# Convolution block: fc2 and projection in four column tiles, the sum in sequence quarters, stored and read back as channels

## What is computed

```python
mid = jax.nn.silu(xn @ fc1_w + fc1_b) @ fc2_w + fc2_b
...
o = o / jnp.linalg.norm(o, axis=-1, keepdims=True)
o = o + mid
o = o.transpose(0, 2, 1, 3).reshape(B, L, Cc)
o = o @ proj_w + proj_b
...
x = x + _L0_conv_ref(_gn(x), ...)
t = _to_tokens(x)
t = t + _L1_attn_ref(_ln_t(t), ...)
t = t + _L1_ffn_ref(_ln_t(t), ...)
```

## Time and profile before

| | |
|---|---|
| time, median of 3 executions | 2920.16 us (2918.62 to 2920.73) |
| profiled execution, its own time | 2919.42 us |
| its span, first to last instruction | 2917.7 us |
| mean granted TensorE clock | 0.977 |
| busy: TensorE / VectorE / ScalarE / GpSimd | 94% / 79% / 69% / 40% |
| convolution block | from about 35 to 1009 us |
| causal attention | to about 2437 us |
| projection and FFN | to the end |

### The profile page before, as it was taken

How to read it: one execution, slowest core, us unless ns; L and a number is a source line. 1 busy time by engine, 2 the same in 40 slices (tenths; PEclk the granted TensorE clock), 3 DMA queues, 4 the chain that set the end, 5 groups by cost and what they waited for, 6 DMA issues and landing times. The chain is left out here.

```text
span 2917.7 us, 86416 instructions
## 1 busy us (share of the span) xinstructions
PE 2750.0 (94%) x29306; PEld 1683.2 (58%) x29306; DVE 2300.3 (79%) x4591; ACT 2020.9 (69%) x3943; POOL 1156.5 (40%) x1999
## 2 busy tenths in 40 slices
PE   3899999999999499999999999999999996899996
PEld 2555555555554266666666666666666664455553
DVE  4576766766666399999999999999999993678997
ACT  1677777777776367777777777777777774577775
POOL 0153434434444444444444444444444431224445
PEclk9999999999999689999999999999999998999998
DMA  1113232332332476666666666666666663334555
GB/s 34 36 63 107 83 113 82 107 110 78 113 113 66 132 127 118 118 117 117 117 117 117 117 117 117 117 117 117 117 117 117 117 114 82 98 99 136 147 139 155
DMA packets 923408, 316.04 MB, mean 108 GB/s; under 512 B 848785, under 2 KB 906418, under 8 KB 923314
## 3 DMA queue, kind: packets, MB, share of 16 engines
q1 hardware_dynamic: 921970, 313.59, 47.6%
q10 hardware_dynamic: 1344, 1.18, 0.1%
HBM read 113.35 MB, written 99.88 MB: 73 GB/s over the span
## 5 line engine op out<-in xcount | busy, mean ns | idle before, releaser
L965 DVE TENSOR_REDUCE at_unit_max<-at_ps_queries 128x1 f32<-128x512 f32 (+4 forms) x2304 | 1135.0, 549 | 89.0 <-PE at_ps_queries L853 86.6
L928 ACT ACTIVATE at_probs<-at_ps_keys 128x512 f32<-128x512 f32 x1344 | 743.3, 603 | 387.6 <-PE at_ps_keys L868 383.0
L853 PE MATMUL at_ps_queries<-at_turned 96*128 96x128 bf16 (+3 forms) x3456 | 634.4, 274 | 33.1 <-DMA at_turned<-at_spread 32.3
L868 PE MATMUL at_ps_keys<-at_turned 128*128 128x128 bf16 (+3 forms) x3456 | 648.7, 275 | 1.8 <-ACT at_probs L928 1.5
L803 POOL TENSOR_TENSOR at_v<-at_stacks,at_one 128x128 f32<-128x128 f32 x192 | 76.9, 401 | 813.0 <-DMA at_stacks<-qkv_rows 813.0
L888 PE MATMUL at_ps_values<-at_probs,at_v 128*32 128x128 f32 x10752 | 373.4, 276 | 6.5 <-ACT at_probs L928 6.4
L868 PEld LDWEIGHTS at_ps_keys<-at_turned 128*128 128x128 bf16 x3456 | 237.8, 97 | 239.5 <-ACT at_probs L928 88.6
L853 PEld LDWEIGHTS at_ps_queries<-at_turned 96*128 96x128 bf16 x3456 | 289.3, 97 | 124.4 <-DMA at_turned<-at_spread 34.0
L888 PEld LDWEIGHTS at_ps_values<-at_probs,at_v 128*32 128x32 f32 x10752 | 269.5, 109 | 120.5 <-ACT at_diag_probs L928 70.2
L928 ACT ACTIVATE at_diag_probs<-at_ps_keys 128x512 f32<-128x512 f32 x384 | 208.6, 595 | 8.2 <-PE at_ps_keys L868 5.3
L822 POOL TENSOR_SCALAR_AFFINE_SELECT at_diag_probs<-at_diag_probs 128x1024 f32<-128x1024 f32 x192 | 210.6, 1097 | 0.0
(11 more groups left out here) (212 smaller groups left out, 5028.3 us busy)
## 6 DMA issues: line engine op xcount, KB each, us to landing
qkv_rows<-cb_packed SPq DMA_DIRECT2D x32, 1536.0 KB, 8.2
at_stacks<-qkv_rows SPq DMA_DIRECT2D x192, 256.0 KB, 3.3
cb_x<-in_x_dram SPq DMA_DIRECT2D x32, 384.0 KB, 3.7
cb_x_again<-in_x_dram SPq DMA_DIRECT2D x32, 384.0 KB, 4.6
x_after_conv<-cb_x SPq DMA_DIRECT2D x32, 384.0 KB, 5.0
attention_rows<-at_att SPq DMA_DIRECT2D x384, 32.0 KB, 2.2
ff_att_rows<-attention_rows SPq DMA_DIRECT2D x32, 384.0 KB, 4.4
ff_x<-x_after_conv SPq DMA_DIRECT2D x128, 96.0 KB, 2.4
```

The lines of the kernel that those rows point to most:

```text
L853: mm = pe.matmul(pq[:, u % QBANKS, c0:c0 + n], QT[0:STACK, slot, qb * P:(qb + 1) * P], KT[0:STACK, slot, k0:k0 + n], start=(c0 == 0), stop ...
L868: mm = pe.matmul(pk[:, bank_k, c0:c0 + n * P], KT[:, slot, kb * P:(kb + 1) * P], QT[:, slot, q0 * P:(q0 + n) * P], start=(c0 == 0), stop=True,
L928: act.activation(probs, pk[:, (slot * NU + k) % KBANKS, :], ACT.Exp, scale=scale).then_inc(S["probs"], 1)
L965: dve.tensor_reduce(peaks, scores, AX.X, ALU.max).then_inc(S["unit_max"], 1)
```

## The change

Four things belong together. The output product is split in 3 channel blocks of 32 (b) and 4 position quarters (t): each matmul has 32 output columns and 256 positions and writes partitions 32 t to 32 t + 31 of PSUM, so `po` then holds all 128 partitions by 3 x 256. The sum on VectorE is made in this shape, from x loaded in the same shape with four DMAs instead of one, into a new buffer X1Q. X1Q is stored to DRAM, where x1 now has the shape of the quarters. From DRAM three DMAs bring it back as 96 channels by 1024 positions into X1 for the second product; SyncE waits for the store to land before it issues them, and TensorE has a new wait for them. VectorE's wait on `a_psum` moves to SyncE. The bias becomes a [128, 3] tile made from four loads and twelve small products. The last stage loads x1 with one DMA instead of four.

```diff
@@ prepare
+        QP = C // 3
+        loads += [(projb[q * QP:(q + 1) * QP, :], A["L0_conv_proj_b"].rearrange("(b c) -> c b", c=QP)) for q in range(4)]
...
-                pe.matmul(bank[4][0:C, 0:1], w["proj"][:, :], fc2b[:, :], start=True, stop=True)
+                for b in range(3):
+                    for q in range(4):
+                        pe.matmul(bank[4][q * QP:(q + 1) * QP, b:b + 1], w["proj"][:, b * QP:(b + 1) * QP], fc2b[:, :],
+                                  start=True, stop=True)
@@ conv_block, SyncE
-                        sp.dma_start(XR[:, (r + 1) % 2, :], x_in[i - 3]).then_inc(xr_loaded[(r + 1) % 2], 16)
+                        for k in range(4):
+                            sp.dma_start(XR[k * QP:(k + 1) * QP, (r + 1) % 2, :, :],
+                                         x_in[i - 3].rearrange("(b c) (k t) -> k c b t", c=QP, t=QT)[k]
+                                         ).then_inc(xr_loaded[(r + 1) % 2], 16)
                     if on(4):
                         sp.wait_ge(S["x1_ready"], i - 3)
-                        sp.dma_start(x1[i - 4], X1[:, r, :]).then_inc(x1_stored[r], 16)
+                        sp.dma_start(x1[i - 4].rearrange("p (b t) -> p b t", b=3), X1Q[:, r, :, :]
+                                     ).then_inc(x1_stored[r], 16)
+                        _above(sp.wait_ge, S["a_psum"], TILES * (i - 5))
+                        sp.wait_ge(x1_stored[r], _dmas(lap, r, 4, 2))
+                        for b in range(3):
+                            sp.dma_start(X1[b * QP:(b + 1) * QP, r, :].rearrange("c (k t) -> c k t", t=QT),
+                                         x1[i - 4].rearrange("(k c) (b t) -> b c k t", c=QP, b=3)[b]
+                                         ).then_inc(x1_loaded[r], 16)
@@ conv_block, VectorE
-                        dve.wait_ge(xr_loaded[q], _dmas(lap, r, 3, 2))
+                        dve.wait_ge(xr_loaded[q], 4 * _dmas(lap, r, 3, 2))
                         _above(dve.wait_ge, x1_stored[q], _dmas(lap, r, 5, 2))
-                        _above(dve.wait_ge, S["a_psum"], TILES * (i - 4))
-                        dve.scalar_tensor_tensor(out=X1[:, q, :], in0=po[0:C, :], scalar=w["out_bias"][:, 0:1],
-                                                 in1=XR[:, q, :], op0=ALU.add, op1=ALU.add).then_inc(S["x1_ready"], 1)
+                        for b in range(3):
+                            ins = dve.scalar_tensor_tensor(out=X1Q[:, q, b, :], in0=po[:, b * QT:(b + 1) * QT],
+                                                           scalar=w["out_bias"][:, b:b + 1], in1=XR[:, q, b, :],
+                                                           op0=ALU.add, op1=ALU.add)
+                        ins.then_inc(S["x1_ready"], 1)
@@ conv_block, TensorE
-                        for a in range(2):
-                            half = slice(a * BANK, (a + 1) * BANK)
-                            for k in range(CHUNKS):
-                                pe.matmul(po[0:C, half], w["fc2"][:, k, :], HT[:, q, k, half], start=(k == 0),
-                                          stop=False)
-                            if a == 0:
-                                pe.wait_ge(S["oht_ready"], i - 2)
-                            mm = pe.matmul(po[0:C, half], w["proj"][:, :], OHT[:, half], start=False, stop=True)
+                        for k in range(CHUNKS):
+                            for b in range(3):
+                                for t in range(4):
+                                    pe.matmul(po[t * QP:(t + 1) * QP, b * QT:(b + 1) * QT],
+                                              w["fc2"][:, k, b * QP:(b + 1) * QP], HT[:, q, k, t * QT:(t + 1) * QT],
+                                              start=(k == 0 and b != 1), stop=False, skip_group_check=True)
+                        pe.wait_ge(S["oht_ready"], i - 2)
+                        for b in range(3):
+                            for t in range(4):
+                                mm = pe.matmul(po[t * QP:(t + 1) * QP, b * QT:(b + 1) * QT],
+                                               w["proj"][:, b * QP:(b + 1) * QP], OHT[:, t * QT:(t + 1) * QT],
+                                               start=False, stop=True, skip_group_check=True)
                         mm.then_inc(S["out_done"], 1)
...
+                        pe.wait_ge(x1_loaded[r], 3 * _dmas(lap, r, 4, 2))
                         for t in range(TILES):
@@ project_and_ffn
-                    for q in range(4):
-                        sp.dma_start(X1[q * QP:(q + 1) * QP, n % 2, :, :], quarters(x1[n])[q]
-                                     ).then_inc(x_loaded[n % 2], 16)
+                    sp.dma_start(X1[:, n % 2, :, :], x1[n].rearrange("p (b t) -> p b t", b=3)
+                                 ).then_inc(x_loaded[n % 2], 16)
```

More of the change, by code:

```diff
@@ L64, in _constants @@
     w["proj"] = sb("proj", [C, C])
-    w["out_bias"] = sb("out_bias", [C, 1])
+    w["out_bias"] = sb("out_bias", [P, 3])
     w["w_attn"] = sb("w_attn", [C, 4 * C])
@@ L96, in prepare @@
         fc2b = sb("fc2b", [C, 1])
-        projb = sb("projb", [C, 1])
+        projb = sb("projb", [P, 3])
         ones1 = sb("ones1", [C, P])
@@ L128, in prepare @@
             (fc2b[:, :], A["L0_conv_fc2_b"].rearrange("(n a) -> n a", a=1)),
-            (projb[:, :], A["L0_conv_proj_b"].rearrange("(n a) -> n a", a=1)),
         ]
+        QP = C // 3
+        loads += [(projb[q * QP:(q + 1) * QP, :], A["L0_conv_proj_b"].rearrange("(b c) -> c b", c=QP)) for q in range(4)]
         NLOADS = len(loads)
@@ L202, in _ @@
                 link(dve.tensor_copy(fc2_t[:, :], bank[3][0:C, 0:HIDDEN]))
-                link(dve.tensor_tensor(w["out_bias"][:, :], bank[4][0:C, 0:1], projb[:, :], ALU.add))
+                link(dve.tensor_tensor(w["out_bias"][:, :], bank[4][:, 0:3], projb[:, :], ALU.add))
                 link(dve.tensor_copy(w["w_attn"][:, :], bank[5][0:C, 0:4 * C]))
@@ L298, in conv_block @@
         X = sb("x", [C, 2, L])
-        XR = sb("x_again", [C, 2, L])
+        QP, QT = C // 3, L // 4
+        XR = sb("x_again", [P, 2, 3, QT])
+        X1Q = sb("x1_quarters", [P, 2, 3, QT])
         X1 = sb("x1", [C, 2, L])
@@ L356, in conv_block @@
         x1_stored = [sem(f"x1_stored{i}") for i in range(2)]
+        x1_loaded = [sem(f"x1_loaded{i}") for i in range(2)]
         rows_stored = [sem(f"rows_stored{i}") for i in range(2)]
@@ L1329, in _ @@
                         dve.wait_ge(S["y_done"], n + 1)
-                        dve.wait_ge(x_loaded[n % 2], 64 * (n // 2 + 1))
+                        dve.wait_ge(x_loaded[n % 2], 16 * (n // 2 + 1))
                         _above(dve.wait_ge, x2_stored[n % 3], 16 * (n // 3))
@@ L1377, in build @@
 def build(nc, A, out):
-    x1 = nc.dram_tensor("x_after_conv", [BATCH, C, L], FP32, kind="Internal").ap()
+    x1 = nc.dram_tensor("x_after_conv", [BATCH, P, 3 * L // 4], FP32, kind="Internal").ap()
     rows = nc.dram_tensor("qkv_rows", [BATCH, L, HEADS * PACK], U32, kind="Internal").ap()
```

## The result

The changed kernel takes 3052.58 us (median of 4 runs, 3048.86 to 3058.63); the kernel before takes 2920.44 us on the same chip. The ratio is 1.0455, with a 95% interval of 1.0435 to 1.0475: 4.6% slower. The forecast was 3039 us with a range of 2985 to 3110. The profiled execution took 3058.6 us, the longest of the four, against 2919.4 us for the profiled one before: 139 us to account for.

A forecast was written before the change was run, and what follows sets the result against it. Full TensorE, with a nearly as long chain through SyncE's issues, the rows' landing and Silu, was taken as the bound. 24 x (3.2 detour + 2.0 clock) = +125, others -5, together +120: 3039 us, range 2985 to 3110.

The forecast's parts named there:

- The product: TensorE's output product in the convolution loop: some 5.2 to 5.4 us instead of 6.87, saving 1.7 us a round.
- VectorE's sum: VectorE's sum in the loop becomes three instructions, covered by 5.33 us of idle time: no cost.
- SyncE's round: Rows issued at T + 7.8, landed at T + 14.4 (T: XS finished on VectorE); rounds 7 to 30 grow 3.2 us.
- The detour: SyncE's x1 store, wait and reload ahead of the rows' store: rounds of 31.2 us instead of 28.0, +3.2.
- The clock: TensorE idle 4.9 us before hidden(i, 1) each round, granted clock falls: 2.0 us more in each of 24 rounds.
- Together: Rounds 7 to 30: 24 x (3.2 + 2.0) = +125 us.
- Rounds 3 to 5: Rounds without rows to store, where the product's saving counts whole: 3 x 1.7 = -5 us.
- Rounds 6, 31 and 32: No loss forecast: from 31 on the detour is hidden, drain 0 within 3 us; round 6 got no term.
- Preparation, start of the last stage, tail: Kernel's ends: preparation +3 us for more issues and tiny matmuls, start of last stage -3, later x1 loads 0.
- The same detour without a lower clock: Rival for rounds 7 to 30: 24 x 3.2 - 5 = +72, 2991 us; chance 0.13.
- TensorE alone: Rival: TensorE alone sets the time, whole saving shows, 32 x 1.7 = -54, 2865 us; chance 0.01.
- The detour is hidden: Rival: rows land by T + 11.2, a round gains at most 0.4 us, -15, 2904 us; chance 0.03.

The follow-up runs named there:

- e5: Changed kernel with SyncE's store of the rows right behind the load of x, and VectorE's cast subtraction behind its two reductions: 2873.68 us, ratio 0.9847.
- e3: Changed kernel with four matmuls of unused result where TensorE idles ahead of hidden(i, 1), in rounds 7 to 31: 2991.54 us, ratio 1.0257.
- e9: Changed kernel with the store of the rows first in SyncE's round, and VectorE's cast subtraction behind its two reductions: 2872.56 us, ratio 0.9841.
- e1: Changed kernel with the store of the rows moved ahead of SyncE's wait for the x1 store, the reload of x1 staying behind it: 2918.88 us, ratio 0.9998.
- e4: Changed kernel with the store of the rows first in SyncE's round, VectorE's order untouched: 2986.33 us, ratio 1.0227.
- e8: Changed kernel with the store of the rows right behind the load of x, VectorE's order untouched: 2980.54 us, ratio 1.0211.

## Why the prediction was right, step by step

- *The product.* 5.39 us against 5.2 to 5.4. The saving is 1.5 us in the product and 1.36 in the round (e5's rounds, and rounds 3 to 5), where hidden(i, 1) takes 3.89 us instead of 3.78; 1.7 had been taken.
- *VectorE's sum.* Hidden, as said; it is three instructions and VectorE is no limit in any run.
- *SyncE's round.* The rows went out at T + 7.8, as worked out. The store of x1 landed in 3.4 us in this round and 3.7 in the median (3.4 taken), the rows in 5.9 (6.6 taken). They landed at T + 13.7 instead of T + 14.4. The detour's own price is therefore 13.7 + 16.8 - 28.0 = 2.5 us, not 3.2. e3, whose clock is nearly full, shows 30.8 - 28.0 = 2.8. The term was oversized by the landing of the rows: with three loads of x1 ahead of them it is 0.3 us over that of the earlier trace rows, where 1.0 had been added.
- *The clock.* It falls in every one of the 24 rounds, as forecast. Its term was undersized, 2.7 us by the trace (6.57 - 3.89) and by e3 (33.5 - 30.8), where 2.0 was taken. The 2.0 was read from one stall, where 5.84 stood against 3.78; the repeated ones take up to 7.09 - 3.78 = 3.3, and that same first stall takes up to 6.85 us in the experiments.
- *Together.* 5.2 us a round were forecast and 5.5 found; 24 rounds gave +133 instead of +125. Two errors, of 0.4 to 0.7 us in the detour and 0.7 in the clock, had opposite signs: the mechanism was right, and that the sum came this close is in part luck.
- *Rounds 3 to 5.* -4.1 instead of -5, the product's saving being smaller.
- *Rounds 6, 31 and 32.* The step that failed. Nothing was foreseen and +8 us came. The prediction had taken idle times of 1.67 us as harmless and 3.36 as harmful, and did not ask what the saving of 1.5 us would add to the 0.8 us of idle already there. It makes 2.33 us, and that is enough. The 1.67 us, too, was read from one place only (below the list).
- *Preparation, start of the last stage, tail.* +2.4 against +3; the rest 0 within 1 us, against -3.
- *A quoted figure.* The 2.0 us fixed that the prediction quotes from the Trainium skill ("DMA: Bandwidth & Descriptors", anatomy of one DMA) is given there for DMAs that GpSimd issues. Here SyncE issues them, and no term of the sum used it.
- *The rivals.* "The same detour without a lower clock" at 2991 us is what e3 makes by force: 2991.5, with a smaller detour than the rival's 3.2 and two rounds at the lower clock. "TensorE alone" at 2865 us is nearly what e5 and e9 reach: 2873, with 1.36 us a round and not 1.7. Both were priced nearly rightly; neither was what this order of instructions does. "The detour is hidden" needed the rows by T + 11.2. e1 makes it so, with the rows at 432.15 - 421.35 = T + 10.8, and its rounds are 0.2 us under those of before, where at most 0.4 had been allowed.

The 1.67 us of idle time was read as harmless from a single row. Another place of the same trace says otherwise. Here are the same eight records after the same idle time, and the busy times of the stretch behind it, with the granted clock as the third number from the end:

```profile
2500.98 1.61 PE L1138 MATMUL ff_ps_turn<-ident,ff_xn 128*96 128x128 f32 x8 [1.67 <-POOL ff_xn L1268]
```
```profile
2501.40:2504.70 3.30, 3.30 (x25) 2.47 (x26) 0.80 (x1) 1.02 (x1) 0.00 (x0) 0.50 0.00 0
```

They take 1.61 us instead of 1.08, at a granted clock of 0.50, the lower of the two levels. So the trace of before already held a fall of the clock after less than 2.33 us of idle.

One thing the prediction's map lacked is the third chain. Behind the late rows lay 1.3 us that VectorE lost beside GpSimd. Removing the late store altogether (e4, e8) recovers only half of the loss until that is mended too.

## What to carry to other kernels

A wait for a round trip through memory costs little by itself, and much to what stands behind it in the same issuing queue: put independent stores ahead of it. Before a faster product is put on a full engine, look at what it will then wait for; a saving that turns into idle time on TensorE can cost more than it was; here 2.33 us of idle were enough. And when a late transfer is mended, look at which engines it had kept apart.

## What the runs showed of the hardware

- An idle time of 2.33 us on TensorE was mostly followed by a lower granted clock: eight records took 5.40, 5.69 and 7.09 us instead of 3.89 in rounds 6, 31 and 32 of the changed kernel, and 5.40 in most rounds of e4 and e8. It was not always so: round 6 of e1, rounds 6 and 32 of e3 and two rounds each of e4 and e8 show 3.89 after 2.33. Shorter idle times went either way too: after 1.67 us in the last stage of the kernel before, eight records took 1.08 us at 2478.66 and 1.61 at 2500.98, where the granted clock was 0.50; in e3 1.80 us was followed by 5.40. So the idle time just ahead does not alone decide it.
- The price of a lower clock after one and the same idle time varies from trace to trace. The stall of 6.09 us in the first round is in all traces; the eight records behind it took 5.84 us before, 5.89 in the changed kernel, 5.72 and 5.74 in e5 and e8, and 6.72 to 6.85 in the seven others. The stalls that return take 5.40 to 7.09 us. One sample at the low end was the basis of the 2.0 us forecast.
- VectorE's 128x1536 subtraction to bf16 took 1.75 us alone and 3.03 beside a GpSimd product that had begun before it. The GpSimd product took 1.47 alone and 2.96 beside a VectorE product that had begun before it. In both cases the extra is about the overlap, as if the second had waited for the first. VectorE's reductions beside the same GpSimd product lost nothing (1.74 us in e1, 0.95 in e9). Which of the two lost went by who began: in e8 a lead of 0.13 us of the one or 0.21 us of the other was enough. What the two share, no run here shows.
- A store of 1536 KB landed in 5.9 us behind three loads of 128 KB, in 7.3 right behind the store of x1 (e1) and in 8.2 before the change (medians).
